# Second batch's tokens, parts and normalisation placed by a table of their own, other places for all steps, and the attention weights elsewhere in the shared tile

## The chip, the cores and the metric

One core of one Trainium2 chip runs the whole kernel in one launch. The metric is the device time of that launch in microseconds (us), lower is better. All times below are us unless marked ns. The engines are PE (TensorE), DVE (VectorE), ACT (ScalarE), POOL (GpSimd) and SP (SyncE, which here only issues DMAs).

## What is computed

Input x is 8 batches of 512 tokens of width 128, float32. Two residual blocks follow each other, each closed by a layer norm:

```python
x = layernorm(x + gated_attention(x))      # 16 heads of 64; a gate keeps 32 of 512 tokens, the others get scores of 0
h = x + causal_attention(rmsnorm(x, g1))   # 16 heads of 8; keys and values out of a latent of 64
t = rmsnorm(h, g2)
h = h + sum over the best 2 of 8 experts of gate_e * (silu(t @ w1[e]) @ w2[e])   # 128 -> 256 -> 128
x = layernorm(h)
```

In the gated attention only 32 tokens of a batch have scores other than 0. The kernel gathers them, so that this block is short, and what it adds to x comes from small tables: a `base` row for each batch and a `delta` row for each of the 32 tokens. The causal attention takes all 512 x 512 scores of 16 heads, in all 8 batches, and all 8 experts are run for every token.

## The kernel before

**Two functions, one after the other.** `gated_attention` (the first 57.8 us of the span) computes gate, top 32, `base` and, for batches 0 to 3, `delta`. `causal_attention_and_experts` does the rest. The gated attention of batches 4 to 7 (steps named `half ...`) is also in it, as filler.

**A list of steps.** In `causal_attention_and_experts` each engine runs one loop over one list, `steps_in_order()` (line 675), and does its share of every step. A step is (what, batch, number) and has a place, a decimal number. The list is sorted by place; places have no other meaning and no time. One slot is 1.0, a batch has 24 slots (4 head groups with 6 weight steps each), so batch b begins at place 24 b. Each engine keeps strictly to the order of the list and waits on semaphores; a step that waits holds up everything behind it on its engine.

**Attention steps.** `score` (PE L1043) writes scores, ten slots ahead of their weights; `maximum` (DVE L1283) takes the row maxima; `shift` (DVE) puts them beside the queries, and `again` turns the queries once more (PE L983, ACT L1145). `weight` (PE L1060) computes transposed scores, and ACT takes their exponential (L1191) into `prob`. PE's next `weight` waits for this exponential. `select` (POOL L886) clears the part above the diagonal, `value` (PE L1072) multiplies by the values. `keys` and `queries` are turned by PE (L983) and copied by ACT.

**Steps of a batch, which the tables place.** The first block's end comes as `rows` (POOL, adds `base`), `apply` (PE L917, DVE L1214: adds `delta`), `deviations` (DVE L1219), `variances` (DVE L1224 to L1235), `first root` (POOL L847, a power of -0.5), `offset` (DVE L1245: minus mean times root) and `normalize` (ACT L1091, four tiles with `offset` as bias). A batch's tokens for the second block then go through `next` (POOL L858), `nextT` (PE L966, ACT L1118), four `qkv` (PE L973) and four `parts` (ACT L1124, L1125, L1134, then DVE L1205, L1207). After attention come `turn`, `attnT`, `project`, `statistics`, `moments`, `root`, `scale`, `tokensT`, `split`, `logits`, `rank`, `compare`, `count`, `combine` (the router), and `residuals` (POOL L880). The experts of batch b run in the slots of batch b+1: `hidden` (PE L1021, ACT L1159), `gate` (DVE L1342), `down` (PE L1028), `sum` (DVE L1361), `add` (POOL L894), closed by `norm`, `norm root`, `result`.

**Where the places stand.** `OF_GROUP`, `OF_BATCH` and `OF_LAST` hold places counted from the batch's begin. `NORMAL_FROM` says from which place a batch's `apply` to `normalize` run, with the distances of `NORMAL`; `EARLY` and `NORMALIZE_EARLY` do so for batches 0 and 1, `OFFSET_EARLY` for batch 1's `offset`. `unread` steps (`UNREAD_AT`) are two matmuls whose result nobody reads.

**Three banks in turn.** All PE steps of the list other than `score`, `weight` and `value` write to one of three PSUM banks in turn, in list order; a step waits until the step three before it in turn has been read.

**Buffers.** `rs1` (roots) and `off1` (offsets) have two buffers, used by batch modulo 2. The tile `prob` is 8192 columns wide; until the causal attention begins it holds the loaded weights `WQKV` and the tokens `XT`, `Xg`, `Xc`:

```python
for name, at, size in (("WQKV", 0, 3 * INNER), ("XT", 3 * INNER, B * T), ("Xg", 3 * INNER + B * T, B * TOPK),
                       ("Xc", 3 * INNER + B * T + B * TOPK, B * TOPK)):
```

Of the kernel before, what the change touches and what calls it, by code (L numbers as in the profile page):

```python
# [674 lines left out]
def steps_in_order():  # L675
# [3 lines left out]
    def put(place, what, b, n):  # L679
        steps.append((place, what, b, n))  # L680

    for b in range(B):
        first = SLOTS * b
        for n in range(NG * SCORE_STEPS):
            slot = first + n - AHEAD
            put(slot + IN_SLOT["score"], "score", b, n)
            put(slot + IN_SLOT["maximum"], "maximum", b, n)
        for n in range(SLOTS):
            put(first + n + IN_SLOT["weight"], "weight", b, n)
        for g in range(NG):  # L690
# [4 lines left out]
            for what, at in OF_GROUP.items():
                put(first + WEIGHT_STEPS * g + at, what, b, g)
        begin, pitch, lead = UNITS.get(b, UNITS["usual"])
        for i, (what, n) in enumerate(expert_units(lead)):
            slot = first + SLOTS + begin + pitch * i
            put(slot + pitch * IN_SLOT["unit"], what, b, n)  # L700
            if what == "hidden":
                put(slot + pitch * GATE_AT, "gate", b, n)
            else:
                put(slot + pitch * SUM_AT, "sum", b, n)
                put(slot + pitch * ADD_AT, "add", b, n)
        for (what, n), at in OF_BATCH.items():
            put(first + (OF_LAST.get((what, n), at) if b == B - 1 else at), what, b, n)
        if b >= ROWS_EARLY:
            put(ROWS_FROM + ROWS_PITCH * (b - ROWS_EARLY), "rows", b, 0)
        for what, at in NORMAL.items():  # L710
# [13 lines left out]
def causal_attention_and_experts(nc, keep, out):  # L724
# [6 lines left out]
    with ctx:  # L731
# [102 lines left out]
        def _(pool):  # L834
            own = Chain(pool, s["own_pool"])
            for what, b, n in order:
# [7 lines left out]
                    pool.tensor_tensor(rs1[:, 0, 0, :], ve1[:, 0, 0, :], mhalf[:, 0:C], ALU.pow).then_inc(s["rs1_ready"], 1)  # L844
                elif what == "first root":
                    pool.wait_ge(s["ve1_ready"], b + 1)
                    pool.tensor_tensor(rs1[:, b % 2, :, :].rearrange("p k c -> p (k c)"),  # L847
                                       ve1[:, b % 2, :, :].rearrange("p k c -> p (k c)"), mhalf[:, :],
                                       ALU.pow).then_inc(s["rs1_ready"], 1)
# [228 lines left out]
        def _(act):  # L1078
            A = nc.scalar.activation

            for what, b, n in order:
# [112 lines left out]
        def _(dve):  # L1194
# [3 lines left out]
            for what, b, n in order:  # L1198
# [38 lines left out]
                elif what == "offset":  # L1237
                    if b == 0:
                        dve.wait_ge(s["both_root"], 1)
                        own(V.reciprocal(both[:, :], both[:, :]))  # L1240
                        for c in range(C):
                            V.tensor_scalar(xr[:, c, :], X[:, c, :], mv1[:, 0, c, 0:1], both[:, c:c + 1], ALU.subtract,
                                            ALU.mult).then_inc(s["xr_first"], 1)
                    dve.wait_ge(s["rs1_ready"], b + 1)
                    V.scalar_tensor_tensor(out=off1[:, b % 2, :], in0=mv1[:, b % 2, :, 0], scalar=-1.0,  # L1245
                                           in1=rs1[:, b % 2, 0, :], op0=ALU.mult,
                                           op1=ALU.mult).then_inc(s["off1_ready"], 1)
                elif what == "half scores":
# [239 lines left out]
```

## Time and profile before

| | us |
|---|---|
| median of 3 runs | 679.62 |
| lowest, highest | 675.57, 682.0 |
| the profiled execution | 679.0 |
| its span, first to last instruction | 677.1 |
| mean granted TensorE clock, share of full | 0.971 |
| PE busy | 637.5 (94%) |
| DVE, ACT, POOL busy | 519.7 (77%), 425.9 (63%), 252.9 (37%) |

The span is read in stages. The gated attention takes 57.8 us; then comes a lead-in to 92.6, in which tokens of batches 0 and 1 are prepared and ten scores are taken ahead; then eight batches; after 616 only the experts of batch 7 and the last rows are left. The first exponentials of batches 0 to 7 start at 93.1, 155.0, 218.8, 288.7, 356.0, 426.9, 493.1 and 557.0. In the text "batch 4's slots" are the 24 slots that begin with batch 4's first weight, whatever other batch the work in them belongs to.

### The profile page before, as it was taken

What the parts mean: (1) busy time and instruction counts of PE and PEld (TensorE: products, weight loads), DVE (VectorE), ACT (ScalarE), POOL (GpSimd) and SP (SyncE); (2) the same over time, 40 slices, a digit from 0 to 9 for tenths busy, and PEclk for the clock granted to TensorE, in tenths of its full rate; (3) what the DMA queues carried; (4) which work ended last, traced back from release to release, by engine and by line L of the source; (5) the groups of instructions that cost most, each with busy time, mean ns of one, the idle gap of its engine ahead of it and who ended that gap; (6) DMA issues with size and microseconds to landing.
All of it is one profiled execution on the core that took longest, in us unless ns stands there. A gap on an engine that the chain in (4) does not pass through costs nothing.

```text
span 677.1 us, 14123 instructions
## 1 busy us (share of the span) xinstructions
PE 637.5 (94%) x5047; PEld 421.2 (62%) x5047; DVE 519.7 (77%) x1814; ACT 425.9 (63%) x777; POOL 252.9 (37%) x320
## 2 busy tenths in 40 slices
PE   7999888998899999899999999999999999999895
PEld 3576444454466676666666566766676667756785
DVE  2756688677788889877988798789887987864675
ACT  3663656575767666757685768675867676674442
POOL 8130612222424353335343434343435253443432
PEclk9999899697999999989999899999999999999988
DMA  8600000000000000000000000000000000000000
GB/s 315 196 19 17 0 1 1 2 1 1 1 1 2 1 1 1 17 1 1 2 16 1 1 2 16 1 3 1 17 1 1 1 16 1 1 1 16 1 16 16
DMA packets 10070, 12.15 MB, mean 18 GB/s; under 512 B 1609, under 2 KB 8210, under 8 KB 9746
## 3 DMA queue, kind: packets, MB, share of 16 engines
q1 hardware_dynamic: 9250, 11.25, 5.0%
q8 instruction: 40, 0.66, 0.4%
q14 instruction: 28, 0.23, 0.1%
q10 hardware_dynamic: 752, 0.01, 0.1%
HBM read 9.16 MB, written 2.10 MB: 17 GB/s over the span
## 4 chain that ended last, share of the span: by engine, by line
PE 65%; DVE 11%; ACT 5%; issue 5%; POOL 2%; POOLq 0%; ACTq 0%; DVEq 0%
PE turn L1028 15%; PE turn L1021 12%; PE psV L1072 11%; PE psW L1060 8%; PE turn L983 5%; DVE psS L1283 4%; PE psS L1043 3%; PE turn L973 3%; PE turn L991 2%; ACT prob L1191 2%; PE turn L1002 1%; ACT X L1091 1%; ACT late L1159 1%; DVE late L1342 1%; PE turn L1013 1%
## 5 line engine op out<-in xcount | busy, mean ns | idle before, releaser
L1191 ACT ACTIVATE prob<-psW 128x1024 f32<-128x1024 f32 (+1 forms) x192 | 183.2, 954 | 106.3 <-PE psW L1060 105.7
L1283 DVE CUSTOM_DVE_ANT_0 psS<-psS,maskb 128x512 f32<-128x512 f32 (+2 forms) x498 | 232.1, 518 | 19.3 <-PE psS L1043 18.6
L886 POOL TENSOR_SCALAR_AFFINE_SELECT prob<-prob 128x512 f32<-128x512 f32 x128 | 80.0, 637 | 221.4 <-ACT prob L1191 217.2
L1028 PE MATMUL turn<-wexp,late 128*128 128x128 f32 x1024 | 129.6, 280 | 0.2 <-DVE late L1342 0.2
L1028 PEld LDWEIGHTS turn<-wexp,late 128*128 128x128 f32 x1024 | 120.9, 193 | 10.1 <-issue 7.5
L1342 DVE SCALAR_TENSOR_TENSOR late<-late,turn 128x512 f32<-128x512 f32 x128 | 87.5, 685 | 46.0 <-ACT late L1159 45.0
L1159 ACT ACTIVATE late<-turn 128x512 f32<-128x512 f32 x128 | 76.4, 597 | 46.9 <-PE turn L1021 42.8
L894 POOL TENSOR_TENSOR late<-late 128x512 f32<-128x512 f32 x62 | 79.5, 1282 | 61.7 <-DVE late L1361 61.7
L1060 PE MATMUL psW<-qT,kT 26*128 26x256 f32 (+2 forms) x512 | 94.2, 404 | 8.6 <-ACT prob L1191 8.0
L1043 PE MATMUL psS<-kT,qT 24*128 24x256 f32 (+1 forms) x498 | 92.3, 406 | 4.5 <-DVE top L1283 3.4
L1072 PE MATMUL psV<-prob,va 128*32 128x512 f32 (+3 forms) x1024 | 93.2, 460 | 0.8 <-POOL prob L886 0.8
L1060 PEld LDWEIGHTS psW<-qT,kT 26*128 26x128 f32 x512 | 43.7, 186 | 80.6 <-issue 56.7
L1283 DVE DVE_READ_ACCUMULATOR2_ANT top<- 128x1 f32 x512 | 72.2, 141 | 0.0
L1361 DVE TENSOR_TENSOR late<-turn,comb 128x512 f32<-128x512 f32 x62 | 42.8, 690 | 36.3 <-PE turn L1028 36.1
L1021 PE MATMUL turn<-tTh,w1h 128*128 128x512 f32 x128 | 63.1, 493 | 2.4 <-DVE late L1361 1.9
L1043 PEld LDWEIGHTS psS<-kT,qT 24*128 24x128 f32 x498 | 42.9, 186 | 13.8 <-DVE top L1283 7.7
L1021 PE MATMUL turn<-tTl,w1h 128*128 128x512 f32 x128 | 51.2, 400 | 0.0
L1021 PE MATMUL turn<-tTh,w1l 128*128 128x512 f32 x128 | 50.9, 398 | 0.0
L1072 PEld LDWEIGHTS psV<-prob,va 128*32 128x32 f32 x1024 | 24.0, 111 | 35.5 <-issue 24.8
L983 PE MATMUL turn<-ident,qs 128*128 128x128 f32 x256 | 41.9, 287 | 4.3 <-DVE qs L1291 3.7
L983 PEld LDWEIGHTS turn<-ident,qs 128*128 128x128 f32 x256 | 28.2, 143 | 15.1 <-issue 10.6
L1021 PEld LDWEIGHTS turn<-tTh,w1h 128*128 128x128 f32 x128 | 24.2, 189 | 19.4 <-issue 10.9
(272 smaller groups left out, 883.5 us busy)
## 6 DMA issues: line engine op xcount, KB each, us to landing
prob<-in_xT SPq DMA_DIRECT2D x4, 512.0 KB, 6.4
X<-in_x SPq DMA_DIRECT2D x1, 2048.0 KB, 16.3
out<-late SPq DMA_DIRECT2D x8, 256.0 KB, 2.2
prob<-in_wqkvT SPq DMA_DIRECT2D x1, 1024.0 KB
late<-in_w SPq DMA_DIRECT2D x1, 1024.0 KB, 9.6
prob<-in_wqkvT SPq DMA_DIRECT2D x2, 256.0 KB, 3.5
late<-in_woutT SPq DMA_DIRECT2D x1, 512.0 KB
oT<-base_rows SPq DMA_DIRECT2D x2, 256.0 KB, 3.1
```

Source lines behind the costliest of these rows:

```text
L886: pool.affine_select(out=blk, in_=blk, compare_op=ALU.is_ge, fill=0.0, base=0, pattern=[[0, 4], [1, P]], channel_multiplier=-1).then_inc(s ...
L894: pool.tensor_tensor(acc[:, b % 2, :, :], acc[:, b % 2, :, :], prod[:, n % 2, :, :], ALU.add).then_inc(s["prod_used"], 1)
L983: last = tr(into[:, P * c:P * c + P], stack[:, b % 2, c, 4 * n:4 * n + 4, :].rearrange("p h r -> p (h r)").bitcast(F32), ident[:, :])
L1021: last = mm(into[:, :], w[:, e, P * k:P * k + P], v[:, :], start=(i == 0), stop=(i == 2))
L1028: last = mm(into[:, D * c:D * c + D], hid[:, n % 2, k, P * c:P * c + P], wexp2[:, n, k, :], start=(k == 0), stop=(k == 1))
L1043: last = mm(scores_in(b, n)[:, j, HALF * i:HALF * i + keys], qT[row:row + SHIFT, u % 2, P * c:P * c + P], kT[row:row + SHIFT, g, 0:keys], ...
L1060: last = mm(psW[:, j, HALF * i:HALF * i + T - q0], kT[row:row + SHIFT + 2, g, P * kc:P * kc + P], qT2[row:row + SHIFT + 2, u % 2, q0:T], s ...
L1072: last = mm(psV[R * a:R * a + R, P * kc:T], va[:, kc, 4 * g + a, :], prob[:, kc, a, P * kc:T], start=(kc == 0), stop=(kc == C - 1), tile_p ...
L1159: A(tanh[:, n % 2, :], bank("hidden", b, n)[:, :], ACT.Tanh, scale=0.5).then_inc(s["tanh_ready"], 1)
L1191: A(into, src, ACT.Exp).then_inc(s["exp_ready"], 1)
L1283: last = V.tensor_tensor_reduce(at, at, maskb[:, T - P * (c + 1):T], 1.0, BIG, ALU.add, ALU.max, top[:, u % 2, c, 2 * p + j:2 * p + j + 1])
L1342: V.scalar_tensor_tensor(out=hid[:, e % 2, k, :], in0=tanh[:, n % 2, :], scalar=1.0, in1=bank("hidden", b, n)[:, :], op0=ALU.add, op1=ALU. ...
```

## The change

- `rs1` and `off1` get four buffers (batch modulo 4).
- Batch 1's `next`, `nextT`, `qkv` and `parts` get a table `OF_SECOND`: they move from the lead-in (places -13.05 to -2.59) to places -6.85 to 5.61, among batch 0's first weights.
- Batch 0's `normalize` moves from place -8.35 to 8.5, batch 1's from -9.9 to -1.5.
- The runs from `apply` to `normalize` move: batch 2 from -1.3 to -0.3, batch 3 from 16.7 to 13.7, batch 5 from 40.7 to 39.7, batch 6 from 67.7 to 61.7, batch 7 from 97.7 to 94.7. Batch 4's stays at 22.7. `first root` stands right behind `variances` (1.81 in place of 2.01).
- In every batch: `tokensT` 0.85 earlier, `nextT` 0.65 earlier, `next` 1.1 earlier, `combine` 0.7 later, `turn` 2 0.3 earlier, `qkv` 1 and `parts` 1 one slot and 0.7 later, the first `select` of a group 1.2 earlier and the third and fourth 1.0 and 1.3 later, `add` 0.5 earlier.
- Of the last batch, `residuals` comes before `root`, `sum` 6 of batch 6 before its `rank`; a few others move without changing places with a step of their engine.
- `unread` at 7.8 and 8.8 go, those at -37.7, 27.8 and 57.8 are added: 30 in place of 29.
- `XT` now lies at columns 0 to 4095 of `prob`, `WQKV` behind it. Loads, sizes and their order are as before.

```diff
-GATE_AT, SUM_AT, ADD_AT = 1.0, 1.01, 2.82
+GATE_AT, SUM_AT, ADD_AT = 1.0, 1.01, 2.32
-SELECT_AT = (3.0, 4.0, 4.2, 4.21)
+SELECT_AT = (1.8, 4.0, 5.2, 5.51)
-OF_GROUP = {"keys": -12.05, "queries": -13.55, "shift": -4.1, "again": -3.35, "values": -8.0}
+OF_GROUP = {"keys": -12.05, "queries": -13.2, "shift": -4.1, "again": -3.35, "values": -7.65}
 OF_BATCH = {
-    ("next", 0): -37.05, ("nextT", 0): -31.5, ("qkv", 0): -29.6, ("parts", 0): -29.59, ("qkv", 1): -29.6,
-    ("parts", 1): -29.29, ("qkv", 2): -27.8, ("parts", 2): -27.74, ("qkv", 3): -26.6, ("parts", 3): -26.59,
+    ("next", 0): -38.15, ("nextT", 0): -32.15, ("qkv", 0): -29.8, ("parts", 0): -29.59, ("qkv", 1): -28.6,
+    ("parts", 1): -28.59, ("qkv", 2): -27.65, ("parts", 2): -27.44, ("qkv", 3): -26.6, ("parts", 3): -26.39,
...
+OF_SECOND = {
+    ("next", 0): -30.85, ("nextT", 0): -23.15, ("qkv", 0): -21.8, ("parts", 0): -21.59, ("qkv", 1): -20.6,
+    ("parts", 1): -20.59, ("qkv", 2): -19.3, ("parts", 2): -19.64, ("qkv", 3): -18.6, ("parts", 3): -18.39,
+}
...
-NORMAL = {"apply": 0.0, "deviations": 1.0, "variances": 1.8, "first root": 2.01, "offset": 3.0, "normalize": 3.01}
-EARLY = {0: -41.35, 1: -26.1}
-NORMALIZE_EARLY = {0: -8.35, 1: -9.9}
-NORMAL_FROM = {2: -1.3, 3: 16.7, 4: 22.7, 5: 40.7, 6: 67.7, 7: 97.7}
+NORMAL = {"apply": 0.0, "deviations": 1.0, "variances": 1.8, "first root": 1.81, "offset": 3.0, "normalize": 3.01}
+EARLY = {0: -40.35, 1: -25.75}
+NORMALIZE_EARLY = {0: 8.5, 1: -1.5}
+NORMAL_FROM = {2: -0.3, 3: 13.7, 4: 22.7, 5: 39.7, 6: 61.7, 7: 94.7}
...
-            put(first + (OF_LAST.get((what, n), at) if b == B - 1 else at), what, b, n)
+            own = OF_LAST if b == B - 1 else OF_SECOND if b == 1 else {}
+            put(first + own.get((what, n), at), what, b, n)
...
-        ve1, rs1 = sb("ve1", [P, 2, 2, C]), sb("rs1", [P, 2, 2, C])
+        ve1, rs1 = sb("ve1", [P, 2, 2, C]), sb("rs1", [P, 4, 2, C])
-        rv1, off1 = sb("rv1", [P, 2, C]), sb("off1", [P, 2, C])
+        rv1, off1 = sb("rv1", [P, 2, C]), sb("off1", [P, 4, C])
...
-        for name, at, size in (("WQKV", 0, 3 * INNER), ("XT", 3 * INNER, B * T), ("Xg", 3 * INNER + B * T, B * TOPK),
-                               ("Xc", 3 * INNER + B * T + B * TOPK, B * TOPK)):
+        for name, at, size in (("XT", 0, B * T), ("WQKV", B * T, 3 * INNER), ("Xg", B * T + 3 * INNER, B * TOPK),
+                               ("Xc", B * T + 3 * INNER + B * TOPK, B * TOPK)):
```

## Rows read from the trace of the kernel before

**Rows 1.** The page's part on the chain that ended last, by engine.

```profile
PE 65%; DVE 11%; ACT 5%; issue 5%; POOL 2%; POOLq 0%; ACTq 0%; DVEq 0%
```

**Rows 2.** Windows: stretch, length, busy PE, PEld, DVE, ACT, POOL, PEclk, DMA share, GB/s.

```profile
92.60:106.40 13.80, 10.83 (x126) 5.20 (x126) 10.02 (x47) 8.46 (x13) 3.32 (x5) 0.88 0.00 0
...
218.80:288.70 69.90, 67.23 (x546) 45.48 (x548) 58.98 (x215) 48.38 (x91) 28.44 (x36) 1.00 0.02 5
...
356.00:426.90 70.90, 68.94 (x544) 46.27 (x548) 58.86 (x215) 48.18 (x90) 28.32 (x36) 0.98 0.02 5
426.90:493.10 66.20, 65.78 (x538) 44.42 (x540) 55.70 (x201) 46.84 (x87) 26.84 (x35) 1.00 0.02 6
```

**Rows 3.** Timeline 268 to 293, batch 6's normalisation: start, us, instruction, [idle before <-releaser].

```profile
273.84 0.68 DVE L1214 TENSOR_TENSOR X<-X,turn 128x512 f32<-128x512 f32 x1
...
278.06 0.86 DVE L1219 BATCH_NORM_STATS2 st<-X 128x6 f32<-128x128 f32 x4
...
281.04 0.37 DVE L1224 BATCH_NORM_AGGREGATE mv<-st 128x2 f32<-128x6 f32 x4
...
282.06 0.17 DVE L1235 TENSOR_SCALAR ve<-rv 128x4 f32<-128x4 f32 x1
...
282.32 1.65 POOL L847 TENSOR_TENSOR rs<-ve,mhalf 128x8 f32<-128x8 f32 x1 [8.82 <-DVE ve L1235]
283.93 1.28 POOL L894 TENSOR_TENSOR late<-late 128x512 f32<-128x512 f32 x1
...
284.00 1.24 DVE L1245 SCALAR_TENSOR_TENSOR off<-mv,rs 128x4 f32<-128x4 f32 x1
...
285.27 1.65 ACT L1091 ACTIVATE X<-X,off,rs 128x128 f32<-128x128 f32 x4 [2.36 <-DVE off L1245]
...
287.97 0.50 PE L1060 MATMUL psW<-qT,kT 26*128 26x512 f32 x2 [2.26 <-ACT prob L1191]
```

**Rows 4.** Timeline 366 to 379, PE: the two gaps at batch 7's normalisation.

```profile
372.42 0.51 PE L1021 MATMUL turn<-tTh,w1h 128*128 128x512 f32 x1 [0.86 <-DVE late L1361]
...
374.50 0.54 PE L1060 MATMUL psW<-qT,kT 26*128 26x512 f32 x2 [0.68 <-ACT prob L1191]
```

**Rows 5.** Timeline 141 to 148: batch 3's offset on DVE.

```profile
145.00 0.15 DVE L1245 SCALAR_TENSOR_TENSOR off<-mv,rs 128x4 f32<-128x4 f32 x1
```

**Rows 6.** Windows behind the two normalisations of rows 3 and 4.

```profile
289.50:292.90 3.40, 3.40 (x24) 1.42 (x23) 2.42 (x8) 1.89 (x4) 1.25 (x2) 0.50 0.00 0
...
374.80:378.20 3.40, 3.40 (x19) 1.78 (x15) 2.00 (x5) 2.02 (x4) 2.08 (x3) 0.50 0.00 0
```

**Rows 7.** Timeline 70 to 93, lead-in, ACT and PE.

```profile
73.33 3.19 ACT L1091 ACTIVATE X<-X,off,rs 128x128 f32<-128x128 f32 x8 [1.95 <-DVE off L1245]
...
76.24 0.63 PE L966 MATMUL turn<-ident,xr 128*128 128x128 f32 x4 [2.04 <-POOL xr L858]
...
81.46 1.56 PE L973 MATMUL turn<-wqkv,xrT 128*128 128x384 f32 x4
...
89.17 1.15 PE L917 MATMUL turn<-delta,SR 32*128 32x128 f32 x8
90.26 0.39 PE L921 MATMUL turn<-maskb,identb 128*128 128x512 bf16 x1
...
92.56 0.50 PE L1060 MATMUL psW<-qT,kT 26*128 26x512 f32 x2 [0.36 <-DVE top L1283]
```

**Rows 8.** Window on ACT alone: two of batch 1's four `parts`.

```profile
82.40:84.00 1.60, 1.55 (x6) 1.00 0.00 0
```

**Rows 9.** Timeline 92 to 108, ACT: batch 2's normalisation.

```profile
97.99 1.65 ACT L1091 ACTIVATE X<-X,off,rs 128x128 f32<-128x128 f32 x4 [2.24 <-DVE off L1245]
```

**Rows 10.** Window where batch 6's run now comes to stand.

```profile
254.70:270.00 15.30, 14.92 (x112) 9.10 (x112) 14.50 (x57) 11.31 (x21) 5.54 (x8) 1.00 0.01 2
```

**Rows 11.** Timeline of ACT at the new places of batches 6 and 7.

```profile
266.12 1.02 ACT L1191 ACTIVATE prob<-psW 128x1024 f32<-128x1024 f32 x1 [1.70 <-PE psW L1060]
...
362.54 0.81 ACT L1191 ACTIVATE prob<-psW 128x768 f32<-128x768 f32 x1 [2.78 <-PE psW L1060]
```

More of the change, by code:

```diff
@@ L623 @@
 OF_BATCH = {
-    ("next", 0): -37.05, ("nextT", 0): -31.5, ("qkv", 0): -29.6, ("parts", 0): -29.59, ("qkv", 1): -29.6,
-    ("parts", 1): -29.29, ("qkv", 2): -27.8, ("parts", 2): -27.74, ("qkv", 3): -26.6, ("parts", 3): -26.59,
-    ("turn", 0): 26.65, ("turn", 1): 27.5, ("turn", 2): 29.05, ("turn", 3): 29.8, ("attnT", 0): 30.6,
-    ("project", 0): 31.25, ("statistics", 0): 31.26, ("moments", 0): 31.9, ("root", 0): 32.11, ("scale", 0): 33.25,
-    ("residuals", 0): 40.51, ("tokensT", 0): 35.9, ("split", 0): 35.61, ("logits", 0): 36.25, ("rank", 0): 36.41,
@@ L629 @@
-    ("compare", 0): 36.85, ("count", 0): 38.8, ("combine", 0): 39.61, ("norm", 0): 64.85, ("norm root", 0): 65.31,
+    ("next", 0): -38.15, ("nextT", 0): -32.15, ("qkv", 0): -29.8, ("parts", 0): -29.59, ("qkv", 1): -28.6,
+    ("parts", 1): -28.59, ("qkv", 2): -27.65, ("parts", 2): -27.44, ("qkv", 3): -26.6, ("parts", 3): -26.39,
+    ("turn", 0): 26.3, ("turn", 1): 27.7, ("turn", 2): 28.75, ("turn", 3): 29.8, ("attnT", 0): 30.55,
+    ("project", 0): 31.25, ("statistics", 0): 31.26, ("moments", 0): 31.7, ("root", 0): 32.41, ("scale", 0): 33.25,
@@ L630 @@
+    ("residuals", 0): 40.26, ("tokensT", 0): 35.05, ("split", 0): 35.81, ("logits", 0): 36.55, ("rank", 0): 36.61,
+    ("compare", 0): 36.7, ("count", 0): 38.85, ("combine", 0): 40.31, ("norm", 0): 64.85, ("norm root", 0): 65.26,
     ("result", 0): 67.1,
 }
+OF_SECOND = {
+    ("next", 0): -30.85, ("nextT", 0): -23.15, ("qkv", 0): -21.8, ("parts", 0): -21.59, ("qkv", 1): -20.6,
+    ("parts", 1): -20.59, ("qkv", 2): -19.3, ("parts", 2): -19.64, ("qkv", 3): -18.6, ("parts", 3): -18.39,
+}
 OF_LAST = {
-    ("turn", 0): 26.8, ("turn", 1): 28.1, ("turn", 2): 28.6, ("turn", 3): 28.6, ("attnT", 0): 29.9,
+    ("turn", 0): 27.0, ("turn", 1): 28.1, ("turn", 2): 28.6, ("turn", 3): 28.6, ("attnT", 0): 29.9,
@@ L635 @@
     ("project", 0): 31.45, ("statistics", 0): 31.61, ("moments", 0): 31.7, ("root", 0): 32.11, ("scale", 0): 32.25,
-    ("residuals", 0): 32.61, ("tokensT", 0): 35.6, ("split", 0): 35.26, ("logits", 0): 36.9, ("rank", 0): 35.26,
-    ("compare", 0): 36.4, ("count", 0): 38.3, ("combine", 0): 40.46, ("norm", 0): 64.0, ("norm root", 0): 67.61,
-    ("result", 0): 71.1,
-}
-NORMAL = {"apply": 0.0, "deviations": 1.0, "variances": 1.8, "first root": 2.01, "offset": 3.0, "normalize": 3.01}
-EARLY = {0: -41.35, 1: -26.1}
@@ L643 @@
-NORMALIZE_EARLY = {0: -8.35, 1: -9.9}
-NORMAL_FROM = {2: -1.3, 3: 16.7, 4: 22.7, 5: 40.7, 6: 67.7, 7: 97.7}
+    ("residuals", 0): 30.61, ("tokensT", 0): 35.6, ("split", 0): 35.26, ("logits", 0): 36.9, ("rank", 0): 36.26,
+    ("compare", 0): 36.4, ("count", 0): 39.3, ("combine", 0): 40.46, ("norm", 0): 63.0, ("norm root", 0): 67.61,
+    ("result", 0): 70.1,
+}
+NORMAL = {"apply": 0.0, "deviations": 1.0, "variances": 1.8, "first root": 1.81, "offset": 3.0, "normalize": 3.01}
+EARLY = {0: -40.35, 1: -25.75}
@@ L653 @@
 UNREAD_AT = [
-    -40.12, -40.11, -32.9, -30.0, -9.2, -7.2, -5.2, -1.2, -0.2, 0.8, 1.8, 2.8, 3.8, 7.8, 8.8, 9.8, 11.8, 13.8, 15.8,
-    17.8, 19.8, 22.8, 24.8, 26.8, 29.8, 31.8, 34.8, 37.8, 187.3
+    -40.12, -40.11, -37.7, -32.9, -30.0, -9.2, -7.2, -5.2, -1.2, -0.2, 0.8, 1.8, 2.8, 3.8, 9.8, 11.8, 13.8, 15.8,
+    17.8, 19.8, 22.8, 24.8, 26.8, 27.8, 29.8, 31.8, 34.8, 37.8, 57.8, 187.3
 ]
@@ L846, in _ @@
                     pool.wait_ge(s["ve1_ready"], b + 1)
-                    pool.tensor_tensor(rs1[:, b % 2, :, :].rearrange("p k c -> p (k c)"),
+                    pool.tensor_tensor(rs1[:, b % 4, :, :].rearrange("p k c -> p (k c)"),
                                        ve1[:, b % 2, :, :].rearrange("p k c -> p (k c)"), mhalf[:, :],
@@ L1090, in _ @@
                     for c in range(C):
-                        last = A(X[:, C * b + c, :], X[:, C * b + c, :], ACT.Identity, bias=off1[:, b % 2, c:c + 1],
-                                 scale=rs1[:, b % 2, 0, c:c + 1])
+                        last = A(X[:, C * b + c, :], X[:, C * b + c, :], ACT.Identity, bias=off1[:, b % 4, c:c + 1],
+                                 scale=rs1[:, b % 4, 0, c:c + 1])
                     last.then_inc(s["x_ready"], 1)
@@ L1244, in _ @@
                     dve.wait_ge(s["rs1_ready"], b + 1)
-                    V.scalar_tensor_tensor(out=off1[:, b % 2, :], in0=mv1[:, b % 2, :, 0], scalar=-1.0,
-                                           in1=rs1[:, b % 2, 0, :], op0=ALU.mult,
+                    V.scalar_tensor_tensor(out=off1[:, b % 4, :], in0=mv1[:, b % 2, :, 0], scalar=-1.0,
+                                           in1=rs1[:, b % 4, 0, :], op0=ALU.mult,
                                            op1=ALU.mult).then_inc(s["off1_ready"], 1)
```

2 lines of the change are left out of this document (1 added, 1 removed).

## Prediction

> **What bounds the kernel now.** I read the chain of waits first. PE holds 65% of it, DVE 11%, ACT 5% and "issue" 5% [rows 1]: PE sets the pace, but not alone. Then the windows, cut where a batch's first exponential starts, because a mean over 677 us hides that the stages have different limits. In batch 5's slots PE is busy 65.78 of 66.2 us [rows 2]; nothing in the order of steps can help there, unless PE gets less to do. Batches 2 and 4 take 69.9 and 70.9 us for the same work and one `apply` more [rows 2]. An `apply` costs PE 1.15 [rows 7], so a batch with one should take 66.2 + 1.15 = 67.35. The excess is 2.5 in batch 2 and 3.5 in batch 4.
>
> The timelines show where it comes from. Batch 6's normalisation falls into batch 2's slots: DVE ends `variances` at 282.2, POOL's root takes 1.65, DVE's `offset` 1.24, and ACT, which came to `normalize` 2.36 us before it could begin, needs 1.65 more. Behind it on ACT stands an exponential, for that PE's next `weight` waits, and PE is idle for 2.26 us [rows 3]. Batch 7's, in batch 4's slots, leaves gaps of 0.86 and 0.68 [rows 4]. Each gap has a tail: in 3.4 us soon after each of them the granted clock is 0.50 (1.2 in place of 2.4 GHz), with PE busy throughout [rows 6]. At half clock such a stretch does half the work, so each costs about 1.7. Together: 2.26 + 1.54 + 2 x 1.7 = 7.2 us.
>
> The second place is the start. In the lead-in ACT waits 1.95 for batch 1's offset and then works 3.19 on the tiles of batches 1 and 0; PE stands 2.04 before `nextT` of batch 1, and the first `weight` starts at 92.56 [rows 7]. In the 13.8 us behind it PE is busy only 10.83 and ACT 8.46, at a clock of 0.88 [rows 2]: here is room.
>
> **Part 1, batch 1's tokens out of the lead-in.** PE loses ahead of its first `weight`: the gap of 2.04, `nextT` 0.63 and four `qkv` at 1.56 for two, 3.1 [rows 7], together 5.8. ACT loses the 3.19 of both normalisations there, gets batch 1's 1.65 back at place -1.5, and loses four `parts` at 1.55 for two, 3.1 [rows 8]. What is late next is DVE, whose ten row maxima and batch 2's `apply` now stand close together, and POOL: `next` of batch 1 waits at place -6.85 for a `normalize` at -1.5, and `rows` 6, `rows` 7 and `values` queue behind it; who needs those is the first `heads` at 7.5, far off. I take 5.0 of the 5.8. Bounds: 2.0 (the gap alone) and 5.8.
>
> The work comes back in slots 0 to 6. PE gets 0.63 + 3.1 = 3.7 more; 10.83 + 3.7 = 14.5 against the 13.8 there [rows 2], so at least 0.7 is paid back. ACT gets 3.1 and a copy of about 0.6 more: 8.46 + 3.7 = 12.2, which fits only if it does not wait. Today it waits 2.24 in this stretch for batch 2's offset [rows 9]. In the new list `normalize` of batch 2 stands behind `parts` 0 and `again`, while root and offset stand one slot later too: ACT has something to do meanwhile. I take 1.5 paid back; bounds 0.7 and 3.7. Part 1: 3.5 gained, between -1.7 (2.0 - 3.7) and 5.1.
>
> Batch 0's `normalize` now costs ACT 1.65, as batch 2's does [rows 9], at place 8.5. DVE works on the filler's sums there, not ACT; I take nothing, and 1.65 if the cover is gone.
>
> **Part 2, batch 7's run, 97.7 to 94.7.** ACT comes to `normalize` at the new place just before the stretch in which it waits 2.78 for PE today [rows 11]. `apply`, `deviations` and `variances` bring DVE 0.68 + 0.86 + 1.2 (281.04 to 282.23) = 2.7 [rows 3]. In the old times the offset would be there at about 361.6, `normalize` would take ACT from 361.8 to 363.4, and the exponential due at 362.54 [rows 11] would start 0.9 late, of which PE, with `turn`, `again` and `hidden` ahead of its next wait, feels little: 0.3. What goes is 1.54 and the half clock behind it, 1.7. Part 2: 2.9 gained, between 0.6 (the gap goes, 0.9 comes, the clock still falls) and 3.2.
>
> **Part 3, batch 6's run, 67.7 to 61.7.** This is no empty place. It lies among the router's steps of batch 1, where DVE is busy 14.50 of 15.30 us [rows 10]. Of the 2.7 that the run brings, 0.8 finds room. `offset` stands behind `maximum` and the moved `combine`; in old times DVE comes to it at about 266.8. Then 0.2 + 1.65 for `normalize` and 0.6 for `queries`, which also stands ahead of the exponential: ACT is ready at 269.3. The exponential is due at 266.12 [rows 11] plus the 1.15 of the `apply` that PE now has earlier, 267.3. It comes 2.0 late, and PE's next `weight` feels some 1.8 of that, against 2.26 today; whether the clock falls behind it is open. I count 0.5 gained and keep the clock's 1.7 out; bounds -1.0 and 3.9 (2.26 + 1.7).
>
> Weighed against the Trainium skill. `offset` takes 1.24 in rows 3, where POOL's addition (283.93 to 285.21) ends as it does, and 0.15 where POOL is idle [rows 5]. "SBUF — State Buffer", section "SBUF: two separate sides", calls the port pair that DVE and GpSimd share an exclusive lock that one instruction holds to its end, for DVE operations with two SBUF inputs among others. By that rule, the trace agrees, and it speaks against this place: it is the third rival.
>
> **Part 4, the rest.** Batch 3's and batch 5's runs move by 3 and 1 slots to places like their old ones; batch 4's stays. I take nothing, half a microsecond either way. The `unread` at 57.8 falls into slots where PE is full and costs two matmuls, 0.39 and what the second adds, 0.6 in all [rows 7]; those at -37.7 and 27.8 stand for the ones that go at 7.8 and 8.8: nothing. The steps moved in every batch leave PE the same work. The risk is `tokensT`, whose two ACT copies now stand ahead of an exponential; PE has `down`, `keys` and more between this and its next wait, so nothing, but up to one exponential, 1.02 [rows 11], in each of seven batches if that cover is gone. `select`, `add`, `residuals` and `next` change places on POOL only and hold up nobody by more than they did. Four buffers cost nothing; they allow batch 0's late `normalize`. `WQKV` and `XT` elsewhere in `prob` change neither loads nor waits: all their readers stand ahead of the first exponential on PE, before and after. No DMA moves in its queue.
>
> **Sum**, against the profiled execution, which took 679.0 (its span 677.1 and 1.9 around it) and lies 0.6 under the median of 679.62: 679.0 - 3.5 - 2.9 - 0.5 + 0.6 = 672.7. I say 672.5.
>
> **Rivals.**
> 1. *The start pays all back, and batch 6's place is no better.* Part 1 at 0, parts 2 and 3 at 1.5 together: 679.0 - 1.5 + 0.6 = 678. For it: the 0.7 over in slots 0 to 6 is a floor, and DVE at 14.50 of 15.30 [rows 10]. Against it: the gap of 2.04 and the wait of 2.24 both go. Chance 0.24.
> 2. *Everything falls well.* Part 1 at 5.1, part 3 at 3.9, part 2 at 3.2: 679.0 - 12.2 + 0.6 = 667.4, and less if the clock also holds in batch 0's slots, where it is below 1. Chance 0.15.
> 3. *The offset is caught again.* At batch 6's new place POOL's list has root, `select`, and then `residuals`, a two-input operation like the addition in rows 3, which in old times would run from 266.8, just when DVE comes to `offset`. That adds 1.24 - 0.15 = 1.1 to a stall of 1.8 and makes it larger than today's 2.26: part 3 becomes -0.6, the sum 673.8. Chance 0.12. By the skill's page alone, too, the time would be 673.8.
> 4. *Slower.* The copies of `tokensT` delay the exponential, PE waits up to 1.02 in seven batches: +7.1, and if parts 1 and 2 give only 0.4 together, 686. It decides from the point where PE reaches the second `weight` behind `tokensT` before the exponential of the first has ended; one such wait of 1 us in each batch is enough. Against it: PE is full there today. Chance 0.07.
> 5. *Nothing comes of it*, one stall exchanged for another: within 2 us of 679. Chance 0.07.
>
> **Chances.** The forecast has 0.35, for 669 to 677. 1% of 679.62 is 6.8, about what a measurement of this kernel can tell from no change, so "faster" means under 672.8. That holds for rival 2 (0.15), for a bit over half of the forecast and for a third of rival 3, 0.25 in all, and I add 0.08 for gains in batches 0 and 1 from the clock, which I counted nowhere: 0.48. Slower 0.07. The same 0.45. The range is 664 to 681: below it lies a part of rival 2, above it rival 4 and a little of rival 5.
>
> **What would show it.** Right: the first `weight` near 87.5; ACT's `parts` of batch 1 between its first six exponentials and no wait over 1 us before batch 2's `normalize`; batch 4's slots at 67.4 or less without a window at 0.50; no PE gap over 0.5 around batch 7's `normalize`. Part 3 is right if a gap of 1.5 to 2 us stands before a `weight` in batch 2's slots, some 15 us earlier than today; a gap near 3 speaks for rival 3, if the offset takes over 1 us. Batch 5's slots longer than 67 us would show rival 4. The prediction is wrong if the first `weight` comes later than 90, or if batches 0 and 1 together take more than 128 us.

## The result, and the profile after

In 22 runs each the changed kernel took 676.86 at the median (670.92 to 683.66), the kernel before 680.3 (674.48 to 695.73). The ratio is 0.9948, 95% interval 0.9925 to 0.997: half a per cent faster, a difference that 22 runs resolve and that is smaller than the 1% of the forecast. Medians here are over all runs; the ratios, and the times and clocks "at equal clock" further down, leave out runs over 1.5% above the fastest of their kernel. The profiled execution took 676.7 (span 674.8, granted clock 0.971, as before), 2.3 less than the 679.0 it is set against; the forecast was 6.3 less.

The profile page of after, engine totals, and the line on the chain by engine that answers [rows 1]:

```profile
PE 633.6 (94%) x5032; PEld 422.3 (63%) x5049; DVE 520.1 (77%) x1814; ACT 427.2 (63%) x777; POOL 252.9 (37%) x320
...
PE 67%; DVE 13%; ACT 4%; issue 3%; POOL 1%; POOLq 0%; ACTq 0%; DVEq 0%
```

PE has a little more of the chain, and so has DVE (13 for 11%). The windows show where. First the start, then the slots of batches 2, 3, 4 and 5, as in [rows 2] (stretch, length, busy PE, PEld, DVE, ACT, POOL, PEclk, DMA share, GB/s), then two stretches at half clock (granted clock 0.50, 1.2 in place of 2.4 GHz):

```profile
88.20:102.00 13.80, 12.94 (x90) 6.25 (x91) 10.35 (x50) 10.84 (x23) 3.13 (x4) 0.82 0.00 0
...
216.30:286.40 70.10, 67.13 (x545) 45.25 (x550) 58.12 (x215) 48.56 (x91) 28.35 (x36) 1.00 0.02 5
286.40:354.20 67.80, 66.76 (x544) 45.23 (x548) 56.79 (x205) 47.23 (x86) 26.67 (x35) 1.00 0.02 5
354.20:423.70 69.50, 68.10 (x537) 45.28 (x540) 57.68 (x211) 48.68 (x91) 28.32 (x36) 0.98 0.02 5
423.70:492.10 68.40, 67.35 (x536) 45.05 (x537) 56.13 (x201) 47.11 (x86) 26.64 (x35) 0.98 0.02 6
...
396.80:400.20 3.40, 3.40 (x17) 1.77 (x15) 2.50 (x11) 1.71 (x3) 2.11 (x3) 0.51 0.01 2
465.10:468.50 3.40, 3.40 (x15) 1.88 (x17) 2.40 (x11) 1.89 (x4) 2.11 (x3) 0.50 0.00 0
```

The slots of batch 5, the full ones of before, take 68.4 in place of 66.2, and two new stretches at half clock stand in the slots of batches 4 and 5. Cut at the first exponentials (88.7, 153.0, 216.3, 286.4, 354.2, 423.7, 492.1, 556.3), stage by stage:

| stage | before | after | difference | forecast |
|---|---|---|---|---|
| to the first exponential | 93.1 | 88.7 | -4.4 | -5.0 |
| slots of batches 0 and 1 | 125.7 | 127.6 | +1.9 | +1.5 |
| batch 2 | 69.9 | 70.1 | +0.2 | +0.1 |
| batches 3 and 4 | 138.2 | 137.3 | -0.9 | -2.9 |
| batch 5 | 66.2 | 68.5 | +2.3 | 0 |
| batch 6 | 64.0 | 64.2 | +0.3 | 0 |
| the rest | 120.0 | 118.5 | -1.6 | 0 |
| span | 677.1 | 674.8 | -2.3 | -6.3 |

The forecast is off most where it had no term: in batches 3 to 6, and the other way at the end. PE's gaps there lead to one place. It recurs in the slots of batches 3 to 7; this is the timeline of after in batch 4's (start, us, instruction, [idle before <-releaser]):

```profile
392.53 0.63 POOL L892 TENSOR_SCALAR_AFFINE_SELECT prob<-prob 128x512 f32<-128x512 f32 x1 [3.57 <-ACT prob L1197]
393.13 1.26 POOL L900 TENSOR_TENSOR late<-late 128x512 f32<-128x512 f32 x1
393.29 1.15 DVE L1297 SCALAR_TENSOR_TENSOR qs<-top,qs 128x16 fp32r<-128x16 f32 x1
394.58 0.63 PE L989 MATMUL turn<-ident,qs 128*128 128x128 f32 x4 [0.90 <-DVE qs L1297]
```

And the same place in the kernel before:

```profile
397.55 1.29 POOL L894 TENSOR_TENSOR late<-late 128x512 f32<-128x512 f32 x1 [2.70 <-DVE late L1361]
398.78 0.64 POOL L886 TENSOR_SCALAR_AFFINE_SELECT prob<-prob 128x512 f32<-128x512 f32 x1
398.97 0.49 DVE L1291 SCALAR_TENSOR_TENSOR qs<-top,qs 128x16 fp32r<-128x16 f32 x1
399.61 0.63 PE L983 MATMUL turn<-ident,qs 128*128 128x128 f32 x4 [0.24 <-DVE qs L1291]
```

Before, the `add` of an expert (POOL L894) begins as soon as its `sum` is there and has ended before DVE comes to the second instruction of `shift`; only the shorter `select` runs beside that one, which takes 0.49. After, the first `select`, 1.2 places earlier, stands ahead of this `add`. It waits 3.57 for its exponential, and the `add` starts 0.16 ahead of the second instruction of `shift`. That instruction works on 128x16 elements and takes 1.15; with POOL idle it takes 0.19:

```profile
359.80 0.19 DVE L1297 SCALAR_TENSOR_TENSOR qs<-top,qs 128x16 fp32r<-128x16 f32 x1
```

`again` on PE needs it and waits 0.90 in place of 0.24, in batch 7's slots 1.19 in place of 0.54: some 0.66 in each of five batches. 2.2 after the gap of batch 4 the clock falls (396.8), and shortly behind the same gap of batch 5 it does so again (465.1).

### The profile page after: what moved, and what is told of

The parts are those of the page before. It is cut to its first block, busy times and chain, and to the rows that moved or that the text cites. A ratio compares the mean times of both kernels' runs of the same rounds, so it can differ in the third digit from the quotient of the medians.

```text
span 674.8 us, 14110 instructions
## 1 busy us (share of the span) xinstructions
PE 633.6 (94%) x5032; PEld 422.3 (63%) x5049; DVE 520.1 (77%) x1814; ACT 427.2 (63%) x777; POOL 252.9 (37%) x320
## 4 chain that ended last, share of the span: by engine, by line
PE 67%; DVE 13%; ACT 4%; issue 3%; POOL 1%; POOLq 0%; ACTq 0%; DVEq 0%
PE turn L1034 15%; PE turn L1027 11%; PE psV L1078 11%; PE psW L1066 9%; PE turn L989 5%; DVE psS L1289 5%; PE psS L1049 4%; PE turn L979 3%; PE turn L997 2%; ACT prob L1197 2%; DVE late L1348 2%; PE turn L1019 1%; PE turn L1008 1%; ACT X L1097 1%; DVE late L1367 1%
## 5 line engine op out<-in xcount | busy, mean ns | idle before, releaser
L892 POOL TENSOR_SCALAR_AFFINE_SELECT prob<-prob 128x512 f32<-128x512 f32 x128 | 81.5, 646 | 256.2 <-ACT prob L1197 256.1
L1078 PEld LDWEIGHTS psV<-prob,va 128*32 128x32 f32 x1024 | 23.8, 110 | 37.7 <-issue 23.3
```

What stands on the lines that cost most here:

```text
L892: pool.affine_select(out=blk, in_=blk, compare_op=ALU.is_ge, fill=0.0, base=0, pattern=[[0, 4], [1, P]], channel_multiplier=-1).then_inc(s ...
L1078: last = mm(psV[R * a:R * a + R, P * kc:T], va[:, kc, 4 * g + a, :], prob[:, kc, a, P * kc:T], start=(kc == 0), stop=(kc == C - 1), tile_p ...
```

## The experiments

A small time has to be read here out of a spread of over 10, so first a yardstick. Over the 22 runs of after, time and mean granted clock of a run go together with a correlation of -0.94 and a slope of -421 per unit; 206 of the runs behind the ratios, all kernels together and each run taken about its own kernel's mean, give -425. So 0.01 more of clock is 4.2 less. "At equal clock" below means the mean of a kernel's times, brought with that slope to a clock of 0.971, with two standard errors behind it. It takes out the luck of a run and also what a kernel does to the clock, so both numbers are given. The kernel before, which ran beside every version, is at 679.0, 679.6 and 680.0 at equal clock in three groups of runs, after at 676.0 ± 0.5.

**`a_select`: one `select` put back in after.**

```diff
-SELECT_AT = (1.8, 4.0, 5.2, 5.51)
+SELECT_AT = (3.0, 4.0, 5.2, 5.51)
```

> The changed kernel with the first select of each group back at 3.0, so that POOL again does expert 7's add before it and not behind it. Theory (port): in the changed kernel each batch has a PE gap of 0.90 us before the queries' second turn, because DVE's second shift instruction lasts 1.15 us while POOL's add runs beside it; with the add early the gap is 0.24 again and the instruction 0.49. Five batches by 0.66 is 3.3 us less than the changed kernel, and about 1 us more for each half-clock stretch behind such a gap that goes: 3 to 5 us under the changed kernel, ratio to the kernel before 0.988 to 0.991. Rival (the gap is made by later scores or by tokensT ahead of the exponential): the gap of 0.90 stays and the time is that of the changed kernel, ratio 0.995.

Measured: 672.62, ratio 0.9931 (0.9896 to 0.9965); mean clock 0.9718 against 0.9708 in after; 674.2 ± 0.8 at equal clock, 1.8 ± 0.9 under after. Its timeline at the place:

```profile
393.68 1.29 POOL L900 TENSOR_TENSOR late<-late 128x512 f32<-128x512 f32 x1 [2.90 <-DVE late L1367]
395.11 0.49 DVE L1297 SCALAR_TENSOR_TENSOR qs<-top,qs 128x16 fp32r<-128x16 f32 x1
395.75 0.63 PE L989 MATMUL turn<-ident,qs 128*128 128x128 f32 x4 [0.25 <-DVE qs L1297]
```

The gap is back at 0.25, in all five batches, and with this one number undone the kernel lands on the forecast of 672.5 (in part by luck, as the account of the end below shows).

**`b_select`: the same `select` moved in the kernel before.**

```diff
-SELECT_AT = (3.0, 4.0, 4.2, 4.21)
+SELECT_AT = (1.9, 4.0, 4.2, 4.21)
```

> The kernel before with only the first select of each group at 1.9 in place of 3.0, which puts it between experts 6's and 7's add on POOL. Theory (port): the shift gap grows from 0.24 to 0.90 in five or six batches, ratio 1.004 to 1.007 to the kernel before. Rival (this edit is harmless, something else in the change makes the gap): gap 0.24, ratio 1.000.

Measured: 683.22, ratio 1.0045 (1.0012 to 1.0078), 682.8 ± 0.7 at equal clock: 3 to 4 slower from one number. Here six batches have the gap, those of 2 to 7. The row of the second `shift`, between its neighbours:

```profile
396.69 1.26 POOL L894 TENSOR_TENSOR late<-late 128x512 f32<-128x512 f32 x1
396.85 1.14 DVE L1291 SCALAR_TENSOR_TENSOR qs<-top,qs 128x16 fp32r<-128x16 f32 x1
398.14 0.63 PE L983 MATMUL turn<-ident,qs 128*128 128x128 f32 x4 [0.90 <-DVE qs L1291]
```

The cause is shown in both directions: the gap of 0.90 comes and goes with this place alone. What the 32 second instructions of `shift` in a trace take over their shortest sums to 2.2 before, 4.9 after, 1.6 in `a_select` and 6.1 in `b_select`. The Trainium skill, "SBUF — State Buffer", section "SBUF: two separate sides", has such DVE instructions and POOL's exclude each other until one ends; the rows agree (1.14 to 1.15 behind an addition of 1.26 that began 0.16 earlier).

The 13 traces hold 416 of these instructions. Where no POOL instruction is running as they begin, or one in its last 0.06, they take 0.19 (329 of them). Behind a running addition they take 1.14 to 1.16 (21), behind a running `select`, which reads one tile only, 0.49 to 0.50 (60), and each of these 81 ends 0.04 to 0.05 after POOL's instruction. Beside POOL's `root` of 128x8 elements, 1.65 long, it took 0.21 in all six cases. That one does not hold it, so the rule does not hold beside every POOL instruction here, and the measurement decides.

**`b_second`: Part 1 alone in the kernel before** (four buffers, the table of batch 1, both early `normalize`).

```diff
-NORMALIZE_EARLY = {0: -8.35, 1: -9.9}
+NORMALIZE_EARLY = {0: 8.5, 1: -1.5}
+OF_SECOND = {... as in the change ...}
```

> The kernel before with four buffers for roots and offsets, batch 1's tokens and parts by the new table, and the two early normalisations at their new places; nothing else. My prediction's part 1: first weight 4 to 5 us earlier, 1.5 us paid back in batch 0's first slots, so 3.5 us less, ratio 0.995. Theory after seeing the changed kernel: some 4 us earlier, 2.4 us paid back in batch 0, so 1 to 2 us less, ratio 0.997 to 0.9985. Rival (all is paid back): 1.000.

Measured: 677.85, ratio 0.9987 (0.9959 to 1.0015), 677.0 ± 0.5 at equal clock, 2.1 ± 0.7 under before in the same group of runs. The profiled start is 86.4 (first exponential) and batches 0 and 1 take 129.2. The gain is there at equal clock and not resolved in the raw times, whose clock was 0.9694 against 0.9717 of before.

**`b_norm7` and `a_norm7back`: Part 2 alone, and Part 2 undone.**

```diff
-NORMAL_FROM = {2: -1.3, 3: 16.7, 4: 22.7, 5: 40.7, 6: 67.7, 7: 97.7}
+NORMAL_FROM = {2: -1.3, 3: 16.7, 4: 22.7, 5: 40.7, 6: 67.7, 7: 94.7}
```

> The kernel before with four buffers and batch 7's run from apply to normalize at 94.7 in place of 97.7; nothing else. My prediction's part 2: the gaps of 0.86 and 0.68 go, 0.3 comes, and the half-clock stretch behind them goes: 2.9 us less, ratio 0.9957. If a half-clock stretch costs 1 us and not 1.7, 2.2 us less, 0.997. Rival (the half-clock stretch comes anyway, elsewhere): 1.2 us less, 0.998.

> The changed kernel with batch 7's run from apply to normalize back at 97.7; everything else as changed. If part 2 is worth what the stages of the profiles say, the gaps of 0.86 and 0.68 come back in batch 4's slots and so does a half-clock stretch: 2 to 3 us more than the changed kernel, ratio to the kernel before 0.998 to 0.9995. If the move is worth nothing in time, as the 12 runs of the kernel before with this move alone (0.9998) suggest, 0.995.

Measured: `b_norm7` 679.42, ratio 0.9998 (0.9962 to 1.0035), 679.6 ± 0.8 at equal clock, no gain to be seen where 1.2 to 2.9 were expected. `a_norm7back` 677.13, ratio 0.9973 (0.994 to 1.0006), 677.4 ± 1.0, 1.4 ± 1.1 over after, less than the 2 to 3 expected. In the profiled slots there is more to see. In `b_norm7` batches 3 and 4 take 136.3 for 138.2, a gain of 1.9, of which 1.5 is a stretch at half clock that is gone; its offset fell on POOL's addition:

```profile
370.15 1.22 DVE L1245 SCALAR_TENSOR_TENSOR off<-mv,rs 128x4 f32<-128x4 f32 x1
```

In `a_norm7back` they take 136.8; after takes 137.3, of which 1.55 is the half clock at 396.8. Without that it would be 135.7: Part 2 is worth 1.1 there, since in this profile the clock did not fall behind batch 7's old place, as it did before [rows 6].

**`b_norm6`: Part 3 alone** (6: 61.7 in place of 67.7, and four buffers).

> The kernel before with four buffers and batch 6's run at 61.7 in place of 67.7; nothing else. My prediction's part 3: the gap of 2.26 is exchanged for one of about 1.8 us (1.86 in two pieces in the changed kernel), the half-clock stretch behind it may go: ratio 0.998 to 1.000. Rival (the port holds the offset): gap near 3, ratio 1.001 or more.

Measured: 676.58, ratio 0.9942 (0.9914 to 0.9969), more than the 0.998 to 1.000 expected, but at a clock of 0.9780 against 0.9697 of before; at equal clock 679.1 ± 0.7 against 679.6 ± 0.5. How much of that clock is this version's doing and how much luck stays open. In the profile batch 2 takes 69.14 for 69.87 and batch 3 66.17 for 67.31: a stall smaller by 0.7, and the half clock behind it gone, 1.14. The stall now is three gaps, PE waiting for row maxima; two of its rows:

```profile
261.95 0.50 PE L1043 MATMUL psS<-kT,qT 24*128 24x256 f32 x4 [0.66 <-DVE top L1283]
...
265.46 0.44 PE L1043 MATMUL psS<-kT,qT 24*128 24x384 f32 x2 [0.69 <-DVE top L1283]
```

**`b_layout`: the columns of `WQKV` and `XT` alone.**

> The kernel before with only WQKV and XT in other columns of the shared tile. Both theories: nothing, ratio 1.000, the same gaps on PE. If it moved the time by more than 0.3%, part of what is put down to the moved steps would be its.

Measured: 682.13, ratio 1.0013 (0.9976 to 1.0049), 679.5 ± 0.8 at equal clock against 679.6, with the gaps of before. As forecast, no effect is to be seen.

**`b_last`: the places of `OF_LAST` alone**, to find the 1.6 of the last stage.

```diff
-    ("residuals", 0): 32.61, ... ("rank", 0): 35.26, ("count", 0): 38.3, ("norm", 0): 64.0,
+    ("residuals", 0): 30.61, ... ("rank", 0): 36.26, ("count", 0): 39.3, ("norm", 0): 63.0,
```

> The kernel before with only the last batch's table (OF_LAST) as changed: residuals ahead of root, sum 6 of batch 6 ahead of rank. I counted nothing for it. In the profile of the changed kernel the stretch from batch 7's first exponential to the end is 118.5 us, and 117.8 where the select is back, against 120.0 before with and 119.4 without a half-clock stretch in it. If this table does it, because POOL's add no longer holds up DVE's comparison for 1.1 us, the stretch is 118.4 to 118.8 here and the time 0.9 us less, ratio 0.9985. If the other moved places do it, 119.4 and 1.000.

Measured: 680.78, ratio 1.0019 (0.9983 to 1.0054), 680.1 ± 1.0 at equal clock against 680.0. The profiled stretch from batch 7's first exponential takes 119.8, not the 118.4 to 118.8 expected: a miss. DVE's comparison is free (0.41), and the wait of 0.99 that PE had behind it is 0.54. But with the `add` at its old place `residuals` goes ahead of it on POOL, and `tokensT` waits long for the root:

```profile
647.49 1.28 POOL L880 TENSOR_TENSOR late<-X,late 128x512 f32<-128x512 f32 x1 [7.57 <-DVE late L1303]
648.73 1.29 POOL L894 TENSOR_TENSOR late<-late 128x512 f32<-128x512 f32 x1
...
652.71 0.63 PE L1008 MATMUL turn<-ident,late 128*128 128x128 f32 x4 [2.33 <-POOL late L875]
```

That gap is 1.03 to 1.08 in before and after. That the table pays only together with `add` 0.5 earlier is what these rows suggest; no run shows it.

**`a_best` and `a_best2`: a better version, measured twice.** After with the `select` back, the runs of batches 5 and 6 at places 46.7 and 70.7, and without the `unread` at 57.8.

```diff
-SELECT_AT = (1.8, 4.0, 5.2, 5.51)
+SELECT_AT = (3.0, 4.0, 5.2, 5.51)
-NORMAL_FROM = {2: -0.3, 3: 13.7, 4: 22.7, 5: 39.7, 6: 61.7, 7: 94.7}
+NORMAL_FROM = {2: -0.3, 3: 13.7, 4: 22.7, 5: 46.7, 6: 70.7, 7: 94.7}
...
-    17.8, ..., 37.8, 57.8, 187.3
+    17.8, ..., 37.8, 187.3
```

> The changed kernel with the first select back at 3.0, batches 5's and 6's runs at 46.7 and 70.7 (the place within a batch that batch 7's has), and without the unread at 57.8. Theory: as the changed kernel with the select alone (0.9931), and the gap of 1.53 in batch 2's slots goes as well, and 0.6 of an unread: 2 us less, more if a half-clock stretch goes too; ratio 0.989 to 0.991. Rival (the new places make a wait of their own, as much as they take): 0.993.

> The combination of before once more, as only 6 of its runs counted: ratio 0.982 to 0.988; by the stages 0.987 at equal clock.

Measured: 667.94, ratio 0.982 (0.9777 to 0.9863), and 670.96, ratio 0.9848 (0.9805 to 0.989); at equal clock 670.5 ± 0.8 and 669.9 ± 1.0. The first gained more than the 0.989 to 0.991 expected: batch 2's slots take 68.3 against 72.7 in `a_select`, where 6.8 ran at half clock. Its windows for batches 2 to 5, where [rows 2] has 69.9, 70.9 and 66.2 for batches 2, 4 and 5:

```profile
219.80:288.10 68.30, 67.49 (x544) 45.37 (x547) 57.73 (x215) 48.78 (x90) 28.20 (x36) 1.00 0.02 5
288.10:356.30 68.20, 67.41 (x546) 45.46 (x548) 57.73 (x216) 48.79 (x91) 28.31 (x36) 1.00 0.02 5
356.30:423.50 67.20, 66.40 (x536) 44.42 (x537) 56.84 (x211) 48.58 (x90) 28.19 (x36) 1.00 0.02 5
423.50:489.80 66.30, 65.87 (x538) 44.33 (x540) 55.42 (x201) 47.13 (x86) 26.62 (x35) 1.00 0.02 6
```

No window is below full clock, and each lies within 1.0 of what its work asks for: 66.2, and 1.15 more in batches 2 and 3, which have an `apply`. This version is the fastest of the study, 1.5 to 1.8% under before, 1.3 to 1.5% at equal clock.

**`a_fill`: the gap filled, not removed.** After with six more `unread`, ahead of `again` at the place where PE waits 0.90.

```diff
-    17.8, ..., 57.8, 187.3
+    17.8, ..., 57.8, 62.6, 86.6, 110.6, 134.6, 158.6, 182.6, 187.3
```

> The changed kernel with an unread pair of matmuls just ahead of the queries' second turn in six batches, in the gap of 0.90 that the held-up shift leaves on PE. Nothing is taken away from the wait, only the idle time is filled. If half of such gaps bring 3.4 us at half clock, as the profiles so far show (7 of 16), these stretches go: mean clock up by about 0.002, 2 us less than the changed kernel, ratio to before 0.991 to 0.993, gap 0.3 to 0.5. If the half-clock stretches in batches 3 to 6 fall by chance, whatever the gaps, the time is that of the changed kernel or more, 0.995 to 0.997.

```profile
392.44 1.16 DVE L1297 SCALAR_TENSOR_TENSOR qs<-top,qs 128x16 fp32r<-128x16 f32 x1
393.75 0.63 PE L989 MATMUL turn<-ident,qs 128*128 128x128 f32 x4 [0.37 <-DVE qs L1297]
...
353.40:421.20 67.80, 66.85 (x537) 44.56 (x540) 57.41 (x211) 48.56 (x90) 28.26 (x36) 1.00 0.02 5
421.20:488.20 67.00, 66.42 (x539) 44.56 (x542) 56.10 (x201) 47.23 (x87) 26.80 (x35) 1.00 0.02 6
```

Measured: 673.82, ratio 0.992 (0.9891 to 0.995); mean clock 0.9743 against 0.9708, and 676.2 ± 0.6 at equal clock, as after with 676.0. PE does nothing useful in the filled time, DVE's 1.16 is as long as ever, and yet batches 4 and 5 take 67.8 and 67.0 for 69.5 and 68.4, with no stretch at half clock. The raw gain of 3.0 between the medians is in the clock alone. The interval of the ratio overlaps that of after (0.9925 to 0.997), so this points to the clock and does not prove it by itself.

## Why the prediction was wrong

**The step that failed** is a sentence of Part 4: "`select`, `add`, `residuals` and `next` change places on POOL only and hold up nobody by more than they did". I looked for who waits for these steps' results, and nobody does. What I did not ask is beside which DVE instruction a two-input addition runs once it starts later. I had weighed exactly that for `offset`, in rival 3, and left it out where it recurs batch after batch. The term stood at nothing; measured are 5 x 0.66 = 3.3 of gaps, and two stretches at half clock behind them. In slots with the same work the lengths agree to a few hundredths from batch to batch, so such terms can be read off: slot 15 takes 4.74 and 4.69 in batches 4 and 5, with the half clock, and 3.19 in batch 3, so a stretch costs 1.55 and 1.50.

The bridge from the forecast -6.3 to the measured -2.3: batches 3 to 6 lose 4 x 0.66 + 3.05 = 5.7 (the fifth gap is in the end's number). Against it the half clock that before had in batch 3's slots (1.1) went, and the end gained 1.6 net. Part 1 gave 1.0 less than forecast. 5.7 - 1.1 - 1.6 + 1.0 = 4.0. What is left is small and cancels: batches 3 to 5 are some 0.16 longer each by the other moved steps (66.33 in batch 5's slots of `a_select`, 66.17 before), batch 2 is 0.1 over its forecast, and batch 6's slots are 0.4 shorter. They are so in `a_select` and `a_best` too (63.6) and not in `b_last` (63.9); which moved step does it I can't place. So the term put at nothing, 6.3 with its half clock, is larger than the whole miss of 4.0; what was gained at the end and in batch 3's slots, which I had not counted either, hid part of it by luck.

**Part 1** was right in mechanism and nearly in size. Forecast: 5.0 gained, first weight near 87.5. Timeline of after, the first `weight` and batch 2's `normalize`, which waited 2.24 in [rows 9]:

```profile
87.87 0.79 PE L1066 MATMUL psW<-qT,kT 26*128 26x512 f32 x2
...
95.66 1.65 ACT L1097 ACTIVATE X<-X,off,rs 128x128 f32<-128x128 f32 x4
```

It is 87.87 against 92.56 in [rows 7], although 82.8 to 89.6 ran at half clock. The wait before `normalize` is gone, PE is busy 12.94 of the first 13.8 and not 10.83 [rows 2]. Paid back: 1.9, forecast 1.5. Batches 0 and 1 remain the part that varies: over the profiles batch 2 begins at 213.9 to 219.8 with the new start and at 215.9 to 234.1 with the old, by how much of them is granted at half clock (17 in batch 0's slots in after). Their sum of 127.6 lies just under the 128 that I had named as the limit.

**Part 2**: 2.9 forecast; 2.95 measured between the two profiled executions by comparing each batch 4 slot with the same slot of batch 5 (4.77 over with the run before, 1.82 after, an `apply` in each). The mechanism was as said: at the new place one gap of 0.33 is left, forecast 0.3. The split was 1.4 of wait and 1.5 of clock, not 1.2 and 1.7: batch 4's slots take 69.4 in `b_norm6`, which has the same gaps without the half clock, and 70.9 before. But the clock's part comes only in executions where the clock falls, and `a_norm7back` found 1.1 without it. The term is 1.1 to 2.9, and I had taken its upper end as certain. The sign that I had named for it, batch 4's slots at 67.4 or less without a window at 0.50, did not come: 69.5 with one, by the gap of `shift` and its half clock.

**Part 3**: forecast a stall of 1.8 and an offset not caught. Timeline of after, answering [rows 3] and [rows 11]:

```profile
262.90 1.65 POOL L853 TENSOR_TENSOR rs<-ve,mhalf 128x8 f32<-128x8 f32 x1 [7.01 <-DVE ve L1241]
...
265.12 0.15 DVE L1251 SCALAR_TENSOR_TENSOR off<-mv,rs 128x4 f32<-128x4 f32 x1
265.30 1.65 ACT L1097 ACTIVATE X<-X,off,rs 128x128 f32<-128x128 f32 x4 [2.53 <-DVE off L1251]
...
267.48 0.66 PE L989 MATMUL turn<-ident,ks 128*128 128x128 f32 x4 [1.52 <-ACT qT L1148]
...
268.48 0.49 PE L1066 MATMUL psW<-qT,kT 26*128 26x512 f32 x2 [0.34 <-ACT prob L1197]
```

1.52 + 0.34 = 1.86, as forecast in size. But the waits for row maxima just ahead of them cost too. By whole slots, batch 2 of after is 70.1 - 66.3 - 1.15 - 0.33 = 2.3 over its work (66.3 from `a_select`, an `apply`, an `unread`), before 69.9 - 66.2 - 1.15 = 2.5: 0.3 gained by the unrounded numbers, forecast 0.5; `b_norm6` alone gained 0.7. The larger wait stands before the turned keys, not before the `weight`; it ends with ACT's copy of the queries, queued behind `normalize`. The offset takes 0.15, so rival 3 did not occur in its place. Its mechanism did, elsewhere. The clock, left open, held behind it in this profile: the 1.1 of batch 3's slots. In the profiles of `a_select` and `a_fill` it fell behind the same gap of 1.52 (at 267.5 and 267.0), so that gain is not certain either.

**Part 4, the rest.** `unread` at 57.8 cost 0.33, not 0.6. `tokensT` shows no gap, so rival 4 fell; batch 5's slots are over the 67 that I had named as its sign, but from 0.66 of gap and 1.5 of clock, and are 66.33 in `a_select`. A sign with two causes was badly chosen.

**The end**: 1.6 that I had not seen. Of it 0.66 is the half clock of before at 644.5: `b_norm7` and `b_norm6`, without it, take 119.4 for the stretch, not 120.0. The gap of batch 7 costs 0.64 (118.5 against 117.8 in `a_select`). So the moved steps gain 1.55 here, 0.7 in batch 7's slots and 0.85 behind its last exponential. That is why `a_select` meets the forecast although Part 1 gave less than I said. Before, DVE's comparison was caught by the addition, 1.52 for an instruction that takes 0.41 after:

```profile
639.62 1.34 POOL L894 TENSOR_TENSOR late<-late 128x512 f32<-128x512 f32 x1 [2.31 <-DVE late L1361]
639.72 1.52 DVE L1322 TENSOR_TENSOR equal<-lg 128x256 f32<-128x256 f32 x1
```

```profile
637.60 1.26 POOL L900 TENSOR_TENSOR late<-late 128x512 f32<-128x512 f32 x1 [2.27 <-DVE late L1367]
...
639.18 0.41 DVE L1328 TENSOR_TENSOR equal<-lg 128x256 f32<-128x256 f32 x1
```

PE's wait behind it is 0.99 before and 0.54 after. That this is part of what the end gained is argued from the rows, not shown: `b_last` freed the comparison and did not gain.

**The 2.3 of the profile against 3.4 between the medians** is within what the clock moves: 1.1 is 0.003 of mean clock.

## What to carry to other kernels

When a large POOL operation on SBUF is moved (here the additions and selects of 128x512), that nobody waits for its result is not enough: look beside which short DVE instruction with two SBUF inputs it will run, because that one ends only after it, and ask who waits for DVE. A waiting step moved ahead of a ready one on a strictly ordered engine passes its wait on: here 3.57. Price a repeated step by its repetitions, in both directions of the move. And where PE is nearly full, count a gap of half a microsecond or more with a chance of a stretch at half clock behind it, not as certain and not as nothing.

## What the runs showed of the hardware

**Gaps of PE and the clock.** In the slots of batches 2 to 6, over 13 profiled executions, stretches at half clock stood only at, or up to 2.3 us behind, a gap of PE of 0.5 or more. With gaps of over 2 us (neighbouring ones summed) came one in 6 of 7 cases (in two of them it began 0.6 to 0.7 before the gap's end), of 1 to 2 us in 6 of 10, of 0.5 to 1 us in 6 of 15, and with 17 gaps of 0.3 to 0.5 us in none. In batch 7's slots ten more gaps of 0.5 to 0.7 us brought none, and of three of 1.19 one did. What decides in a single case stays open. A stretch of 3.4 us cost 1.1 to 1.6 in full slots.

**DVE held by POOL.** The 128x16 instruction above: 0.19 free, 0.49 to 0.50 behind a select, 1.14 to 1.16 behind an addition, 0.21 beside the small `root`.

**The spread is the clock.** Most of the spread between runs of one kernel (670.9 to 683.7 in after, correlation -0.94) goes with the mean granted clock. The common slope is -425 per unit; single kernels, with 6 to 32 runs each, give -346 to -557. An effect of 2.1 (`b_second`) shows at equal clock with some 12 runs, where the raw interval still includes 1.
